# Sixteen sequences through a macaron block: the order of every engine's work laid out with other due times and other landing times of the loads

## The reference, cut to what matters

```python
x = x + 0.5 * ffn(layernorm(x))
x = x + attn(layernorm(x))          # 16 heads of 8, causal, T = 256
x = x + 0.5 * ffn(layernorm(x))

def layer(x, ...):                  # twice in each ffn
    q, k, v = split(shift_token(x) @ wqkv)          # 8 heads of 64
    q, k = rotary_xpos(l2norm(q) * qs, l2norm(k) * ksc)
    x = x + local_attention(q, k, v) @ wo           # windows of 64, look back 64
    h = layernorm(shift_token(x)) * lg + lb
    a, g = split(h @ w1 + b1)
    return x + (a * gelu(g)) @ w2 + b2
```

## Time and profile before

| | |
|---|---|
| median of 3 runs | 1858.1 us (1857.13 to 1862.62) |
| profiled execution | 1866.13 us |
| its span, first to last instruction | 1864.3 us |
| mean granted TensorE clock | 0.972 of full speed |
| PE busy | 1680.3 us, 90% |
| ACT busy | 1564.8 us, 84% |
| DVE busy | 1479.3 us, 79% |
| POOL busy | 1286.7 us, 69% |

### The profile page before, as it was taken

One profiled execution on the slowest core, in us unless ns is written; L12 is line 12 of the kernel. 1 busy time (PEld: TensorE's weight loads), 2 busy tenths in 40 slices (PEclk: granted clock), 3 DMA queues, 4 the chain that ended last, 5 costly groups with the idle time before them and its releaser, 6 DMA issues.

```text
span 1864.3 us, 51559 instructions
## 1 busy us (share of the span) xinstructions
PE 1680.3 (90%) x18560; PEld 1367.5 (73%) x18560; DVE 1479.3 (79%) x2938; ACT 1564.8 (84%) x4956; POOL 1286.7 (69%) x1528
## 2 busy tenths in 40 slices
PE   2798899989999999998988899899999999989987
PEld 2577778778877777777777677777687777777776
DVE  5788888688788687888889788876778775788886
ACT  1588799888999898998788888799999887988886
POOL 4899974487394657759998999920559570589991
PEclk9799999999999999999999999999999997999999
DMA  4101000000010000010100011000000000001000
GB/s 113 35 10 24 13 10 11 10 18 19 2 27 11 10 20 14 19 31 18 38 25 24 19 24 28 10 2 2 18 11 19 10 18 1 19 19 28 20 16 15
DMA packets 31701, 36.48 MB, mean 20 GB/s; under 512 B 7986, under 2 KB 18652, under 8 KB 31452
## 3 DMA queue, kind: packets, MB, share of 16 engines
q1 hardware_dynamic: 31452, 33.19, 7.4%
HBM read 5.91 MB, written 2.10 MB: 4 GB/s over the span
## 4 chain that ended last, share of the span: by engine, by line
POOL 37%; PE 23%; DVE 15%; ACT 15%; issue 9%; SPq 1%; DMA 0%; POOLq 0%; ACTq 0%; DVEq 0%
POOL rnorm L1031 13%; POOL parts L1021 11%; POOL parts L1035 8%; ACT probs L1090 8%; PE bank L1427 6%; PE bank L1510 4%; DVE parts L1358 4%; PE bank L1586 3%; POOL sums_floor L1028 3%; ACT turned L1108 2%; POOL rstd L1009 2%; DVE neg_max L1264 2%; PE bank L1546 2%; DVE sums L1365 2%; PE bank L1627 1%
## 5 line engine op out<-in xcount | busy, mean ns | idle before, releaser
L1090 ACT ACTIVATE probs<-bank,neg_max 128x128 f32<-128x128 f32 (+1 forms) x1536 | 584.7, 446 | 36.5 <-DVE neg_max L1264 35.5
L1021 POOL TENSOR_TENSOR parts<-parts 128x256 f32<-128x256 f32 x512 | 377.4, 763 | 161.8 <-DVE parts L1358 160.9
L1031 POOL TENSOR_TENSOR rnorm<-sums_floor,neg_half 128x8 f32<-128x8 f32 x256 | 431.9, 1687 | 21.3
L1090 ACT ACTIVATION_READ_ACCUMULATOR probs<-bank,neg_max 128x1 f32 x1536 | 401.5, 268 | 0.0
L1358 DVE TENSOR_TENSOR parts<-bank,rope 128x1024 f32<-128x1024 f32 x256 | 308.8, 1215 | 51.0 <-ACT squares L1137 49.7
L1264 DVE TENSOR_REDUCE neg_max<-bank 128x4 f32<-128x512 f32 (+1 forms) x448 | 287.5, 681 | 73.5 <-PE bank L1479 39.8
L1035 POOL TENSOR_TENSOR parts<-parts,rnorm 128x512 f32<-128x512 f32 x256 | 278.7, 1089 | 37.6 <-POOL rnorm L1031 1.3
L1510 PE MATMUL bank<-ident,probs 128*128 128x128 f32 x1792 | 253.5, 283 | 39.9 <-DVE probs L1279 19.4
L1108 ACT ACTIVATE turned<-bank 128x512 f32<-128x512 f32 x448 | 258.3, 661 | 34.1 <-PE bank L1510 33.5
L1510 PEld LDWEIGHTS bank<-ident,probs 128*128 128x128 f32 x1792 | 205.4, 145 | 78.3 <-issue 33.3
L1007 POOL TENSOR_SCALAR var_eps<-mean_var 128x2 f32<-128x2 f32 x112 | 32.3, 289 | 318.6 <-DVE mean_var L1297 313.6
(11 more groups left out here) (119 smaller groups left out, 3873.4 us busy)
## 6 DMA issues: line engine op xcount, KB each, us to landing
between<-val SPq DMA_DIRECT2D x192, 128.0 KB, 2.3
x_sb<-in_L_attn_x_dram SPq DMA_DIRECT2D x16, 128.0 KB, 2.7
out_dram<-x_sb SPq DMA_DIRECT2D x16, 128.0 KB, 1.9
raw_qkv<-in_L_ffn_wqkv_dram SPq DMA_DIRECT2D x2, 768.0 KB, 5.5
raw_w<-in_L_ffn_w_dram SPq DMA_DIRECT2D x2, 341.0 KB, 4.3
wo<-in_L_ffn_wo_dram SPq DMA_DIRECT2D x2, 256.0 KB
rope<-in_rope_dram SPq DMA_DIRECT2D x1, 256.0 KB, 3.0
w<-in_L_ffn_w_dram SPq DMA_DIRECT2D x2, 128.0 KB
```

Of the source, the lines that this page charges most:

```text
L1021: last = nc.gpsimd.tensor_tensor(joined[:, :, dst], joined[:, :, dst], sines[:, :, src], ALU.add)
L1031: nc.gpsimd.tensor_tensor(rnorm[:, u], sums_floor[:, u], neg_half[:], ALU.pow).then_inc(sems["pool_step"], 1)
L1090: last = nc.scalar.activation(probs[:, u, block:block + wide].rearrange("p b j -> p (b j)"), bank[:, at:at + P * wide], ACT.Exp, bias=neg_ ...
```

## The change

Only numbers of the planner change: START_AT, STRETCH, PATIENCE, DUE and PHASE_DUE have other values, LATER, which was empty, gets one for each of the 16 sequences and 11 phases, and COME has four more entries and other times. COME is shown whole, of the rest a line or two:

```diff
-STRETCH = 2.094
-PATIENCE = (0.08, 0, 0, 0.37, 0, 0)
+STRETCH = 3.068
+PATIENCE = (0, 0.11, 0, 0.12, 0, 0)
...
-LATER = {}
+LATER = {(0, 0): -5.58, (0, 1): 39.72, (0, 2): 107.33, (0, 3): 9.32, (0, 4): -16.18, (0, 5): -120.89, (0, 6): 34.25,
...
-COME = {("READY", 0, 0): 10.0, ("READY", 2, 0): 9.0, ("READY", 6, 0): 19.0, ("READY", 12, 0): 19.0,
-        ("READY", 21, 0): 37.0, ("FOLD", 0, 0): 13.0, ("FOLD", 1, 0): 13.0, ("FOLD", 2, 0): 37.0, ("FOLD", 0, 1): 23.0}
+COME = {("LNX", 0, 0): 8.5, ("READY", 0, 0): 10.0, ("READY", 2, 0): 9.0, ("READY", 6, 0): 19.5, ("READY", 12, 0): 19.5, ("READY", 15, 0): 19.5, ("READY", 18, 0): 19.5,
+        ("READY", 21, 0): 37.0, ("FOLD", 0, 0): 14.0, ("FOLD", 1, 0): 14.0, ("FOLD", 2, 0): 37.0, ("FOLD", 0, 1): 23.0}
```

More of the change, by code:

```diff
@@ L131 @@
 SHIFT = 3.0
-START_AT = (202.6, 273.5, 93.5, 363.6, 175.9, 399.6, 543.1, 498.0, 1131.2, 1241.1, 1043.6, 1269.8, 1080.2, 1123.5,
-            1215.8, 869.9)
-STRETCH = 2.094
-PATIENCE = (0.08, 0, 0, 0.37, 0, 0)
-DUE = {("FOLD", 0, False): -100.36, ("FOLD", 1, False): -60.02, ("LNH", 0, False): -163.8, ("LNH", 1, False):
-       -86.14, ("LNH", 2, False): -151.56, ("LNT", 0, False): -44.51, ("LNT", 1, False): 22.79, ("LNT", 2, False):
-       -46.32, ("LNX", 0, False): -31.73, ("LNX", 1, False): 41.36, ("MASKS", 0, False): -194.96, ("N", 0, False):
[11 rows of a table removed]
-       ("XADD", 1, False): -183.8}
-PHASE_DUE = {0: 73.98, 1: -99.9, 2: 58.46, 3: -84.9, 4: 22.02, 5: 26.1, 6: -54.71, 7: -53.02, 8: 136.79, 9: 115.74,
-             10: 147.61}
-LATER = {}
+START_AT = (-19.0, 27.1, -190.5, 194.7, -100.0, 87.5, 327.6, 184.0, 900.1, 1165.0, 725.4, 1032.7, 729.7, 825.8,
+            894.0, 536.3)
+STRETCH = 3.068
+PATIENCE = (0, 0.11, 0, 0.12, 0, 0)
+DUE = {("FOLD", 0, False): 36.7, ("FOLD", 1, False): -19.47, ("LNH", 0, False): -236.43, ("LNH", 1, False): -170.18,
+       ("LNH", 2, False): -302.87, ("LNT", 0, False): -49.76, ("LNT", 1, False): 149.91, ("LNT", 2, False): -40.54,
+       ("LNX", 0, False): -90.9, ("LNX", 1, False): 57.5, ("MASKS", 0, False): -189.81, ("N", 0, False): -1.8, ("N",
[11 rows of a table added]
+       ("XADD", 1, False): -184.93}
+PHASE_DUE = {0: 56.35, 1: -89.7, 2: 93.22, 3: -226.74, 4: -5.78, 5: -20.67, 6: -22.69, 7: -12.35, 8: 161.09, 9:
+             113.23, 10: 122.85}
+LATER = {(0, 0): -5.58, (0, 1): 39.72, (0, 2): 107.33, (0, 3): 9.32, (0, 4): -16.18, (0, 5): -120.89, (0, 6): 34.25,
[26 rows of a table added]
 STORING = 6.5
```

## The result

The changed kernel took 1856.6 us (median of 20 runs, 1854.9 to 1860.5); the kernel before, in 20 runs beside it, 1864.5 (1857.1 to 1871.8). The ratio is 0.9958, with a 95% interval of 0.9945 to 0.9971: faster by 0.42%, 7.9 us. Timed once more among the experiments it was 1857.4, and before 1859.5: 0.9986 (0.9971 to 1.0002), by itself not clear of no difference. Over all runs of this study the medians are 1862.3 us (101 runs of before) and 1856.7 (31 of the change), 5 to 6 us apart. The forecast had said 18, and 1840 us. The way was right and the size was not. That 1856.6 still lies within the stated 1808 to 1860 owes nothing to the sum: the upper end was drawn to take in the case of no change.

A forecast was written before the change was run, and what follows sets the result against it. It took the bound to change along the program: GpSimd in Q-heavy pieces, TensorE and ScalarE in the others, VectorE's load wait delaying the start. 12.9 + 3.6 + 1.2 = 17.7 us off 1858.1 gave 1840 us, range 1808 to 1860.

The forecast's parts named there:

- The other thirteen: Of twenty 113-step pieces of TensorE's order, those besides the first, last and five with 17 or 18 Q: 87.4 us each.
- The second rival: Pieces behind the start average 88.7 instead of 87.4 us, 18 us return, 1858 us, no difference; chance 0.12.
- The head: At the start, VectorE's 10.01 us wait for weight loads goes, so Q and GpSimd begin earlier: 12.9 us, bounds 8.8 and 17.8.
- the 4.1 us: At the fifth Q, GpSimd has one scaling (3.1) and one rstd (1.0) more behind it than before; added to 8.8 us.
- The balance: Behind the first piece, four long Q-heavy pieces instead of five: 5.7 us less, 2.1 off for one more Q, leaving 3.6 us.
- The tables: ScalarE's order has 102 table loads instead of 108, 7.7 us of ScalarE, priced by its 15% chain share at 1.2 us.
- The rival of the half clock: In attention over all keys, TensorE's clock stays at half through long lengths without large products, 29 us more each; chance 0.12.

The follow-up runs named there:

- casts_late: The kernel before with only the six raw_wf cast steps moved behind the products of the fourth Q: 1852.3 us, ratio 0.9947.
- before_more: The kernel before with only its start rearranged, fold behind the second Q, raw_wf casts spread over VectorE's gaps between 89 and 200 us: 1851.8 us, 0.9958.
- after_again: The changed kernel unaltered, timed once more beside the follow-up versions: 1857.4 us, ratio 0.9986 to before.
- after_more: The changed kernel with its start taken further: fold behind the second Q, fifth Q earlier, raw_w1 passes later, raw_wf casts and splits spread: 1859.4 us, 0.9992.
- late_warm: The kernel before with the raw_wf casts moved, plus 18 extra TensorE products of 512 columns in the stretch at 1550 us: 1852.0 us, 0.9952.

## Why the prediction was wrong in its size

**The step that failed** is "The other thirteen are what is left of 1850.2 us: 1136.3, or 87.4 each", taken for the new order's pieces as if it were a property of the work: fourteen at 87.4 us and four at 385.0 together, 5.7 us less than before, and no term for waits that the new order brings with it. The fourteen took 88.4 each, 14 us more, and the four 374.6, 10.4 less, so the inner pieces as a whole took 1612.4 us, against 1608.6 forecast and before's 1614.3; the last piece took 1.8 us more, which was put at nothing. The length of a piece is one of the order: laid by the same planner from other numbers, the inner pieces took 1677 and 1693 us. And before's 1614.3 has the stretch at half clock in it. With the old order behind the first piece and less of that stretch they took 1608 (casts_late) and 1600 (before_more), against 1612 to 1615 in the three profiles of the new order (the change, after_again, after_more). So the new order is longer there by 4 to 15 us, although it has six table loads less. Of the 9.7 us at the end of the first piece some 6 are left in the medians. The second rival, "the middle gives the head back", had this mechanism and nearly its size (88.7 us for each of the fourteen), with a chance of 0.12. Where exactly these waits lie is open: it isn't the meetings of VectorE with GpSimd, nor the start, nor the mean clock (0.973 in the change over all runs and 0.971 in casts_late).

**The head (12.9 us) stands, as a size.** All of its times up to the fifth Q came within 0.6 us, the first piece was 8.7 us shorter and ended 9.7 earlier with one Q more in it (10.8 by the prediction, which took 2.1 off for that Q), and undoing the casts alone cost 12.1 us at its end. Two of its reasons don't stand. The casts took 1.14 and 1.30 us and not 3.06, with GpSimd's power (L1057) beside them for the most part; in casts_late, where a scaling and two rope additions stood beside them, they took 3.06:

```profile
31.34 3.06 DVE L1224 TENSOR_SCALAR raw_wf<-high 128x32 f32<-128x32 f32 x12
```

What they saved, others lost. And the 4.1 us for work that stands elsewhere in GpSimd's order assumed that GpSimd leads; after_more, where GpSimd began earlier and nothing was gained, speaks against it. That the sum came out so near all the same is in part luck. The same move is worth less in the old order: in casts_late the first piece ended 6.4 us earlier, with a granted clock of 0.84 in it instead of 0.88.

**The balance (3.6 us) has no ground.** The prediction took two kinds of pieces, 95.6 us with 17 or 18 Q and 87.4 with fewer, and counted one dear piece less. But the lengths are spread without such a step: of the change's pieces with 13 to 15 Q, cheap by the prediction, three took 91.4 to 92.1 us and two 87.9 and 88.5. A straight line can be laid through them too, 80.5 us + 0.73 for each Q through before's eighteen inner pieces and 81.3 + 0.66 through the change's, with much scatter about it (correlations 0.59 and 0.71). Both orders have 224 Q steps in these pieces, so by such a line nothing is gained.

**The tables (1.2 us) were probably too small.** Added loads cost 78 us for 66.5, so by an estimate six fewer would be 7.7 to 9 us. No run takes loads away, and what was taken from GpSimd and VectorE gave back less than one for one.

**The basis was off.** The median stood at 1858.1 from three runs; 101 runs give 1862.3. From the profiled execution 8.0 us were taken off for the difference, and 4 would have been right for before. The change's profiled execution is at its median, 1856.3 and 1856.6 us, so of the 16.6 us between 1840 and the result the 8.0 are one half, and the span, forecast at 1846.6 us and measured at 1854.5, the other.

**The rival of the half clock** had its mechanism right for before, which gains and loses by it from run to run, and not for the change's profiled execution: its longest lengths kept the clock, and no piece behind the first is below 0.94.

**The best kernels** of the study are before with six casts moved (1852.3 us, 0.9947) and, no different by their intervals, before_more (1851.8) and late_warm (1852.0): all with the old order behind the start and none of the change's new numbers.

## What to carry to other kernels

Where four in-order queues feed each other this closely, don't price an engine's microsecond by its share of the chain or its idle time: measure it by adding work. Here an added one cost 0.96 to 1.17, part of it by way of TensorE's clock, and one taken away gave back about half. Before an order is laid anew, try the one move that the waits ask for: here it gave as much as the whole new order or a little more, and a new order has waits of its own in its middle that no count of steps foretold. Don't sort pieces into kinds when the length may as well be a line in what you count. And take the median before from as many runs as the result will have.

## What the hardware showed beyond that

A VectorE instruction with two SBUF operands (128x1024, 1.226 us alone) ran to 2.1 us and GpSimd's power from 1.65 to 2.7 where they met, and taking 128 of the former out made these kernels 41 to 51 us shorter; with a reduction over the same elements in their place GpSimd's lengthened instructions were down to 7.7 us in all. Before's runs lie between 1852.0 and 1872.3 us with nothing changed, and go with the granted clock, 0.981 to 0.964.
